# A four-engine transformer block: GpSimd rounds the feed-forward weights, one bias comes as a late column, and all instruction orders are laid anew

## What is computed

```python
# attention-like part
def _mlp(x, w1, b1, w2, b2): return _gelu(x @ w1 + b1) @ w2 + b2
n  = _ln(x, ln_g, ln_b)
W1 = _mlp(n, h1_w1, h1_b1, h1_w2, h1_b2)          # 128 -> 512 -> 128
W2 = _mlp(n, h2_w1, h2_b1, h2_w2, h2_b2)
W3 = jnp.tril(jnp.einsum('bzn,bsn->bzs', W1, W2))
t  = _ln(_gelu(jnp.einsum('bzs,bsm->bzm', W3, n)), ln_g, ln_b)
x1 = x + t
out = x + _mlp(_ln(x1, ln_g, ln_b), fm_w1, fm_b1, fm_w2, fm_b2)
# feed-forward part; the weights hold only -1, 0, 1, the *_s are scales by output feature
h = silu(tlin(x, w1_w, w1_s)) * tlin(x, w2_w, w2_s)
h = gelu(tlin(h, h1_w, h1_s)); h = gelu(tlin(h, h2_w, h2_s)); y = tlin(h, w3_w, w3_s)
# the block
x = x + _layernorm(attn(_layernorm(x)));  x = x + _layernorm(ffn(_layernorm(x)))
```

## Time and profile before

| | us |
|---|---|
| median of 3 runs | 365.95 (365.81 to 366.39) |
| span of the profiled execution, first to last instruction | 362.6 |
| the median less the span | 3.4 |
| PE busy in the span | 350.1 (97%) |
| DVE busy | 319.9 (88%) |
| ACT busy | 305.2 (84%) |
| GpSimd busy | 147.2 (41%) |

### The profile page before, as it was taken

The page is one execution under the profiler, slowest core; times in us unless marked ns, Lnnn a source line. Parts: engine busy times, 40 slices in busy tenths (PEclk is TensorE's granted clock), DMA queues, the critical chain, the costliest instruction groups (busy, mean ns, idle before and its releaser), DMA issues.

```text
span 362.6 us, 6039 instructions
## 1 busy us (share of the span) xinstructions
PE 350.1 (97%) x1788; PEld 289.2 (80%) x1788; DVE 319.9 (88%) x954; ACT 305.2 (84%) x552; POOL 147.2 (41%) x213
## 2 busy tenths in 40 slices
...
DMA packets 8804, 9.08 MB, mean 25 GB/s; under 512 B 577, under 2 KB 6722, under 8 KB 8770
## 3 DMA queue, kind: packets, MB, share of 16 engines
...
## 4 chain that ended last, share of the span: by engine, by line
PE 67%; ACT 13%; DVE 10%; issue 5%; DMA 2%; POOL 1%; SPq 1%; POOLq 0%; DVEq 0%; ACTq 0%
PE bank L1224 8%; PE bank L1226 8%; PE bank L1240 6%; PE bank L1241 6%; PE bank L1123 4%; PE bank L1104 4%; PE bank L1108 4%; PE bank L1105 4%; PE bank L1120 4%; PE bank L1121 4%; PE bank L1206 4%; PE bank L1209 4%; ACT h_hidden_hi L510 3%; PE bank L1046 2%; ACT bank L515 2%
## 5 line engine op out<-in xcount | busy, mean ns | idle before, releaser
L715 DVE TENSOR_TENSOR ffn_gate_lo<-bank,ffn_gate_hi 128x512 fp32r<-128x512 f32 (+1 forms) x72 | 44.1, 626 | 6.0 <-ACT bank L584 4.9
L510 ACT ACTIVATE h_hidden_hi<-bank,cols 128x512 fp32r<-128x512 f32 x64 | 46.1, 760 | 3.5 <-PE bank L1108 3.2
L515 ACT ACTIVATE bank<-bank,cols 128x512 f32<-128x512 f32 x64 | 45.1, 739 | 0.3
L715 DVE TENSOR_TENSOR h_hidden_lo<-bank,h_hidden_hi 128x512 fp32r<-128x512 f32 x64 | 43.0, 681 | 2.5 <-ACT bank L515 2.5
L584 ACT ACTIVATE bank<-bank,cols 128x512 f32<-128x512 f32 (+1 forms) x72 | 43.7, 620 | 0.7
L1224 PE MATMUL bank<-ffn_gate_hi,ffn_w_hi 128*128 128x512 f32 (+1 forms) x108 | 40.5, 381 | 0.2 <-DVE ffn_gate_lo L715 0.2
L1226 PE MATMUL bank<-ffn_gate_lo,ffn_w_hi 128*128 128x512 f32 (+1 forms) x108 | 39.3, 370 | 0.2 <-DVE ffn_gate_lo L715 0.2
L578 ACT ACTIVATE ffn_h_hi<-bank,cols 128x512 fp32r<-128x512 f32 (+1 forms) x36 | 23.0, 646 | 13.5 <-PE bank L1226 8.3
L578 ACT ACTIVATE ffn_gate_hi<-bank,cols 128x512 fp32r<-128x512 f32 (+1 forms) x36 | 23.2, 647 | 10.6 <-PE bank L1226 8.3
L364 POOL TENSOR_TENSOR XR<-X,ln_x_r 128x512 f32<-128x512 f32 x8 | 8.3, 1042 | 53.6 <-DVE bank L861 53.4
L715 DVE TENSOR_TENSOR ffn_h_lo<-bank,ffn_h_hi 128x512 fp32r<-128x512 f32 (+1 forms) x36 | 22.0, 626 | 8.0 <-ACT bank L584 7.8
...
## 6 DMA issues: line engine op xcount, KB each, us to landing
raw<-ffn_w SPq DMA_DIRECT2D x5, 512.0 KB, 3.9
...
```

The source lines that it names most:

```text
L510: nc.scalar.activation(dst, bank(f"{L}u{j}", c)[:, :], ACT.Gelu, bias=bias_of(L, j)).then_inc(*hi[L].done(c, j))
L515: nc.scalar.activation(u[:, :], u[:, :], ACT.Gelu, bias=bias_of(L, j)).then_inc(*act2[L].done(c, j))
L715: return nc.vector.tensor_tensor(dst, whole, high.bitcast(f32), ALU.subtract)
```

## The change

Four things are done.

- `ffn_w_hi` moves from ACT to GpSimd, as `tensor_copy` (six instructions). Behind each stand the blocks that it feeds.
- `fm_b2` is loaded as a column of 128 values of 4 bytes, straight into its tile. The DMA is issued after `x_piece(2)` in place of before `x_piece(1)`. The two 1x1 matmuls and DVE's copy are gone; `fm_evict(0)` waits for the DMA.
- All orders are laid anew, on all engines, and with them `TURNS`. On PE `fm_bias_product` comes after `down_mm("h1", 2, 0)`; `n_transpose(1)` comes before the last of the h2 layer; `down_mm("h2", 3, 3)` comes before the branch.
- Among what is laid anew is what GpSimd runs around DVE's `n_first` and `n_second`; there `t_r(0)` and `n_low(1)`, for instance, have changed neighbours.

```diff
-        b2_row = M[0:1, 0, :]
...
-            sp.dma_start(b2_row, rows[2:3, :]).then_inc(b2_in, 16)
             x_piece(1, 1, 2)
             for i in (3, 4, 5):
                 attn_piece(i)
             x_piece(2, 2, 3)
+            sp.dma_start(fm_b2[:, :], rows[2:3, :].rearrange("o d -> d o")).then_inc(b2_in, 16)
...
+            def ffn_w_hi(i):
+                c0, c1, at = F_PIECES[i]
+                pool.wait_ge(ffn_in[i], 16)
+                nc.gpsimd.tensor_copy(Fw[0][:, c0:c1], raw[:, at:at + c1 - c0]).then_inc(*ffn_hi.done(0, i))
...
-            x_s_(0); n_low(0); x_s_(1); x_s_(2); lo_block(0); lo_block(1); x_r(0); xr_scale(0); lo_block(2); xr_b(0)
-            lo_block(3); n_low(1); t_r(0); x_r(1); lo_block(4); lo_block(5); x1_r(0); lo_block(6); lo_block(7); x_s_(3)
-            lo_block(8); n_low(2); t_r(1); xr_scale(1); xr_b(1); lo_block(9); o_r(0); x_r(2); x1_r(1); lo_block(10); y_r(0)
+            x_s_(0); n_low(0); x_s_(1); ffn_w_hi(0); lo_block(0); x_s_(2); x_r(0); ffn_w_hi(1); lo_block(1); lo_block(2)
+            xr_scale(0); xr_b(0); ffn_w_hi(2); n_low(1); t_r(0); lo_block(3); lo_block(4); lo_block(5); x1_r(0)
+            ffn_w_hi(3); x_r(1); ffn_w_hi(4); lo_block(6); x_s_(3); ffn_w_hi(5); lo_block(7); n_low(2); t_r(1); x_s_(4)
+            lo_block(8); xr_scale(1); xr_b(1); lo_block(9); o_r(0); lo_block(10); x1_r(1); x_r(2); y_centre(0); y_r(0)
...
-            up_act("h2", 1, 0); up_hi("h2", 3, 0); nT_high(1); up_act("h2", 2, 0); up_act("h2", 3, 0); ffn_w_hi(0)
-            attn_w_hi(5); down_hi("h1", 0); down_hi("h2", 0); up_hi("h1", 0, 1); up_hi("h2", 0, 1); ffn_w_hi(1)
+            up_hi("h2", 2, 0); up_act("h2", 1, 0); up_act("h2", 2, 0); up_hi("h2", 3, 0); up_act("h2", 3, 0); nT_high(1)
+            down_hi("h1", 0); attn_w_hi(5); down_hi("h2", 0); up_hi("h1", 0, 1); up_hi("h2", 0, 1); up_hi("h1", 1, 1)
...
-                nc.vector.tensor_scalar(fm_b2[:, :], bank("fb", 0)[:, J:J + 1], 1.0, None, ALU.mult)
...
-            x_st(0); x_ag(0); n_first(0); n_second(0); attn_w_lo(0); attn_w_lo(1); nT_low(0); x_st(1); x_ag(1); n_first(1)
-            attn_w_lo(2); attn_w_lo(3); up_lo("h1", 0, 0); up_lo("h1", 1, 0); n_second(1); up_lo("h1", 2, 0); up_lo("h2", 0, 0)
-            x_st(2); up_lo("h1", 3, 0); x_ag(2); up_lo("h2", 1, 0); nT_low(1); up_lo("h2", 2, 0); up_lo("h2", 3, 0)
-            attn_w_lo(4); down_lo("h1", 0); down_lo("h2", 0); attn_w_lo(5); fm_bias_add(); score_mask(0, 0); score_mask(1, 0)
-            score_lo(0, 0); score_lo(1, 0); up_lo("h2", 0, 1); up_lo("h1", 0, 1); up_lo("h1", 1, 1); up_lo("h1", 2, 1); x_st(3)
-            t_st(0); n_first(2); t_ag(0); n_second(2); up_lo("h2", 1, 1); t_gain(0); up_lo("h1", 3, 1); nT_low(2); x1_sum(0)
+            x_st(0); x_ag(0); n_first(0); n_second(0); attn_w_lo(0); attn_w_lo(1); nT_low(0); x_st(1); x_ag(1)
+            attn_w_lo(2); n_first(1); n_second(1); up_lo("h1", 0, 0); up_lo("h1", 1, 0); x_st(2); up_lo("h1", 2, 0)
+            attn_w_lo(3); up_lo("h2", 0, 0); up_lo("h1", 3, 0); attn_w_lo(4); up_lo("h2", 1, 0); x_ag(2)
+            up_lo("h2", 2, 0); up_lo("h2", 3, 0); nT_low(1); down_lo("h1", 0); down_lo("h2", 0); attn_w_lo(5); x_st(3)
+            score_mask(0, 0); score_mask(1, 0); score_lo(0, 0); score_lo(1, 0); up_lo("h2", 0, 1); up_lo("h1", 0, 1)
+            up_lo("h1", 1, 1); gate_constants(); up_lo("h1", 2, 1); x_ag(3); t_st(0); t_ag(0); n_first(2)
+            up_lo("h2", 1, 1); n_second(2); up_lo("h1", 3, 1); t_gain(0); nT_low(2); x1_sum(0); up_lo("h2", 2, 1)
...
-                pe.wait_ge(b2_in, 16)
-                last = nc.tensor.matmul(bank("fb", 0)[:, J:J + 1], b2_row, ones[0:1, :], start=True, stop=True)
```

More of the change, by code:

```diff
@@ L436, in _ @@
[L436 to L440, removed]
@@ new lines, in _ @@
+            ffn_w_hi(3); x_r(1); ffn_w_hi(4); lo_block(6); x_s_(3); ffn_w_hi(5); lo_block(7); n_low(2); t_r(1); x_s_(4)
+            lo_block(8); xr_scale(1); xr_b(1); lo_block(9); o_r(0); lo_block(10); x1_r(1); x_r(2); y_centre(0); y_r(0)
+            y_scale(0); o_shift_(0); n_low(3); o_r(1); xr_scale(2); xr_b(2); t_r(2); n_low(4); x1_r(2); y_r(1)
+            y_centre(1); y_scale(1); x_r(3); x_s_(5); o_shift_(1); xr_scale(3); t_r(3); xr_b(3); f_r(0); x_r(4); x1_r(3)
+            o_r(2); y_centre(2); y_r(2); y_scale(2); f_r(1); xr_scale(4); t_r(4); xr_b(4); x_end(0); o_shift_(2); o_r(3)
@@ new lines, in _ @@
+            x1_r(4); x_s_(6); n_low(5); y_r(3); x_r(5); y_centre(3); y_scale(3); o_shift_(3); o_r(4); xr_scale(5); xr_b(5)
+            x_r(6); x_s_(7); y_centre(4); y_r(4); t_r(5); y_scale(4); n_low(6); x1_r(5); x_end(1); f_r(2); f_r(3)
+            x_end(2); xr_scale(6); o_shift_(4); o_r(5); t_r(6); xr_b(6); x_end(3); x_r(7); y_centre(5); y_r(5); y_scale(5)
+            o_shift_(5); n_low(7); x1_r(6); xr_scale(7); o_r(6); xr_b(7); t_r(7); f_r(4); y_centre(6); y_r(6); y_scale(6)
+            o_shift_(6); x1_r(7); o_r(7); o_shift_(7); y_r(7); y_centre(7); y_scale(7); f_r(5); x_end(4); f_r(6); x_end(5)
@@ L445, in _ @@
+            x_shift(); x_end(6); last_rstd(0); last_rstd(1)
         @block.scalar
@@ L609, in _ @@
-            attn_w_hi(5); down_hi("h1", 0); down_hi("h2", 0); up_hi("h1", 0, 1); up_hi("h2", 0, 1); ffn_w_hi(1)
-            up_act("h2", 0, 1); score_hi(0, 0); up_hi("h1", 1, 1); score_hi(1, 0); up_hi("h1", 2, 1); up_act("h1", 0, 1)
-            up_act("h1", 1, 1); up_act("h1", 2, 1); n_high(1); t_act(0); lo_sum(0); lo_sum(1); up_hi("h2", 1, 1); ffn_w_hi(2)
-            up_act("h2", 1, 1); up_hi("h1", 3, 1); up_hi("h2", 2, 1); up_act("h1", 3, 1); nT_high(2); ffn_w_hi(3)
-            up_act("h2", 2, 1); up_hi("h2", 3, 1); down_hi("h1", 1); up_hi("h1", 0, 2); up_act("h2", 3, 1); ffn_w_hi(4)
@@ L689, in _ @@
[L689 to L693 removed]
+            rows_out(); attn_w_hi(0); attn_w_hi(1); attn_w_hi(2); nT_high(0); n_high(0); attn_w_hi(3); up_hi("h1", 0, 0)
@@ new lines, in _ @@
+            up_act("h1", 2, 1); t_act(0); n_high(1); up_hi("h2", 1, 1); lo_sum(0); up_act("h2", 1, 1); up_hi("h2", 2, 1)
+            up_hi("h1", 3, 1); up_act("h1", 3, 1); up_hi("h2", 3, 1); up_act("h2", 2, 1); nT_high(2); up_act("h2", 3, 1)
+            lo_sum(1); up_hi("h1", 0, 2); down_hi("h1", 1); up_act("h1", 0, 2); up_hi("h1", 1, 2); up_hi("h1", 2, 2)
+            up_act("h1", 1, 2); up_act("h1", 2, 2); down_hi("h2", 1); up_hi("h2", 0, 2); lo_sum(2); mT_high(0)
+            up_act("h2", 0, 2); score_hi(0, 1); up_hi("h1", 3, 2); up_hi("h2", 1, 2); score_hi(1, 1); up_hi("fm", 0, 0)
@@ new lines, in _ @@
+            up_act("h1", 3, 2); up_act("fm", 0, 0); up_act("h2", 1, 2); t_act(1); n_high(2); up_hi("fm", 1, 0)
+            up_act("fm", 1, 0); up_hi("h2", 2, 2); up_hi("fm", 2, 0); up_act("h2", 2, 2); up_act("fm", 2, 0)
+            up_hi("fm", 3, 0); up_hi("h2", 3, 2); up_act("fm", 3, 0); up_act("h2", 3, 2); lo_sum(3); nT_high(3)
+            fm_evict(0); down_hi("h1", 2); up_hi("h1", 0, 3); up_hi("h1", 1, 3); up_act("h1", 0, 3); up_act("h1", 1, 3)
+            lo_sum(4); down_hi("h2", 2); up_hi("h1", 2, 3); up_hi("h1", 3, 3); up_act("h1", 2, 3); up_act("h1", 3, 3)
@@ new lines, in _ @@
+            up_hi("h2", 0, 3); up_hi("h2", 1, 3); lo_sum(5); up_hi("h2", 2, 3); up_act("h2", 0, 3); up_act("h2", 1, 3)
+            mT_high(1); up_act("h2", 2, 3); up_hi("h2", 3, 3); score_hi(0, 2); down_hi("h1", 3); up_act("h2", 3, 3)
+            score_hi(1, 2); up_hi("fm", 0, 1); up_hi("fm", 1, 1); up_act("fm", 0, 1); n_high(3); yT_high(0)
+            up_act("fm", 1, 1); down_hi("h2", 3); up_hi("fm", 2, 1); gate_tanh(0, 0); t_act(2); up_hi("fm", 3, 1)
+            gate_tanh(1, 0); up_act("fm", 2, 1); gate_hi(0, 0); up_act("fm", 3, 1); gate_hi(1, 0); nT_high(4)
@@ L971, in _ @@
-            up_lo("h1", 3, 2); t_st(1); up_lo("fm", 0, 0); n_first(3); up_lo("fm", 1, 0); n_second(3); t_ag(1)
-            up_lo("fm", 2, 0); up_lo("h2", 2, 2); up_lo("fm", 3, 0); t_gain(1); nT_low(3); x_st(5); branch(0)
-            up_lo("h2", 3, 2); o_st(0); down_lo("h1", 2); up_lo("h1", 0, 3); down_lo("h2", 2); o_ag(0); x1_sum(1)
-            up_lo("h1", 1, 3); x1_st(1); up_lo("h2", 0, 3); x1_ag(1); up_lo("h1", 2, 3); x_branch(0); m_norm(1); y_st(0)
-            up_lo("h1", 3, 3); y_ag(0); up_lo("h2", 1, 3); mT_low(1); score_mask(0, 2); up_lo("h2", 2, 3); score_mask(1, 2)
@@ new lines, in _ @@
+            yT_low(0); up_lo("fm", 1, 1); n_first(4); down_lo("h2", 3); gate_1(0, 0); n_second(4); gate_1(1, 0)
+            gate_2(0, 0); up_lo("fm", 2, 1); gate_2(1, 0); up_lo("fm", 3, 1); gate_lo(0, 0); gate_lo(1, 0); gate_1(2, 0)
+            nT_low(4); score_mask(0, 3); gate_2(2, 0); gate_1(3, 0); score_lo(0, 3); gate_lo(2, 0); gate_2(3, 0); t_st(2)
+            gate_lo(3, 0); score_mask(1, 3); branch(1); score_lo(1, 3); o_st(1); o_ag(1); t_ag(2); layer_lo("a", 0, 0)
+            up_lo("h1", 0, 4); t_gain(2); layer_lo("a", 1, 0); x_branch(1); layer_lo("a", 2, 0); up_lo("h1", 1, 4)
```

515 lines of the change are left out of this document (255 added, 260 removed), and 45 rows, old and new, of the table TURNS.

## The result

The changed kernel takes 368.67 us (median of 5 runs, 368.18 to 371.01) beside 365.81 us for the kernel before on the same chip (median of 5, 363.63 to 366.39). The two medians are 2.9 us apart; the ratio taken over all of these runs is 1.0109, 95% interval 1.0076 to 1.0142, and stands for 4.0 us. The forecast was 364.0 us, range 361.7 to 366.8. The profiled execution has a span of 366.9 us, 4.3 more than before. In all five runs of the changed kernel the time is 1.7 to 1.8 us above the span, not 3.4; so the profiled execution of the kernel before (span 362.6) was probably one of about 364.4 us, faster than its median, and spans overstate the loss a little.

The account below looks back on a forecast made before the run. ACT was taken to bound the first stage, DVE close behind, and PE the rest. A gain of 2.2 us less 0.25 for shared reads gave 2.0 us, so 364.0 us, range 361.7 to 366.8.

Parts of the forecast that it names:

- What bounds the kernel: From 10 to 73 us ACT is full with DVE close behind; from 73 to 281 us PE is the bound.
- ACT's relief: Roundings leaving ACT between 20.8 and 58.7 us free 5.2 us there; 2.2 us gained, limited by DVE's 3.8 us idle.
- GpSimd's copies: Six roundings on GpSimd, 1.5 us per 1024 columns (1.0 to 2.1): from 20 to 52 us full, but not late.
- The shared reads: DVE's attn_w_lo(5) and one n_second would likely meet GpSimd reads of SBUF: 0.25 us lost, bound 1.3 us each meeting.
- rival D: GpSimd copies block attn_w_lo(5), n_second(1) and n_second(2) on DVE, 1.3 us each, 3.9 in all: 367.7 us, chance 0.13.
- The new orders: All engines' new orders carry the same work: taken as 0, at most 0.7 us won or about 0.8 lost.
- The bias column: Dropping bias work on PE and DVE off the chain, with a hidden DMA: taken as 0, earlier DMAs 0 to 0.4.
- After 73 us: PE is nearly always busy; the stage only starts earlier if the first ends earlier, some 2 us.
- The base and its spread: Profiled span 362.6 us, median 365.95 us, their 3.4 us difference kept; earlier runs spread by 0.58 us.

Follow-up runs that it names:

- e11: The changed kernel with the six roundings back at their old places on ScalarE, plus the two moves of e4: 366.86 us, ratio 1.0042 to the kernel before.
- e6: e4 with one wait more, so that GpSimd begins its first rounding only when n_second(1) has ended: 363.35 us, ratio 0.994 to the kernel before.
- e4: The changed kernel with GpSimd's x_r(1) ahead of lo_block(3) and VectorE's n_second(2) ahead of up_lo(h2,1,1): 364.18 us, ratio 0.998 to the kernel before.
- f2: The kernel before with only the six roundings moved to GpSimd, each right ahead of its first block, other orders kept: 364.81 us, ratio 0.9977.
- e3: The changed kernel with the six roundings back at their old places on ScalarE: 369.95 us, ratio 1.0131 to the kernel before.

## Why the prediction was wrong

- **What bounds the kernel: right. ACT's relief: right in kind, too small by over a third.** ACT lost 5.5 x 0.95 us of work, and e11 against e6 puts the worth of that at 3.7 us, where the forecast had 2.2; that is close to its bound, DVE's 3.8 us of idle time. The 2.2 us between e11 and e4 match the forecast by chance, since the meeting of `n_second(1)` is taken off them. The worth is there only where the orders can use it: f2, in the old ones, had 0.8.
- **GpSimd's copies: the mechanism right, the size below the estimate.** 1.04 us for 1024 columns and 0.61 for 512 (estimate 1.5, bounds 1.0 to 2.1). `n_low(1)` ended at 32.53 us, forecast 32.1. The Trainium skill's figure ("GPSIMD Engine Reference", section 3.1) would have given an estimate of 1.54 us; the measurement decides. In the changed kernel GpSimd was not late; f2 alone shows VectorE waiting for it, 0.5 us more than before.
- **The shared reads, taken at 0.25 us: this step failed.** The runs put the two meetings at 4.7 us (the change against e4, with the clock) and 1.5 us (e4 against e6). It failed in four ways. The price was 0.25 us, taken from one row in which an instruction began 0.39 us before a block ended; the bound, one whole GpSimd instruction, was the price. The count was one price for each step, where a step has four instructions and each can pay: five lost 0.78 and 1.08 us at 12.7 to 15.1, and 0.93, 1.00 and 1.00 us at 34.9 to 38.7, 4.8 us together. `attn_w_lo(5)`, which I had counted on, lost nothing, since it began first and GpSimd's block waited instead (3.02 us for two). And the place was misread: against rival D stood that `n_second(2)` has the short `t_r(0)` beside it. `up_lo` stands ahead of it, and when that was done `t_r(0)` had ended 0.1 us before. The order could have told it: three blocks follow one another there. Last, the readers were the wrong ones: the forecast counted the six moved roundings, but it was three blocks, on GpSimd before and after, that held `n_second(2)`, and e3 has that meeting without a rounding on GpSimd. The Trainium skill's rule ("SBUF — State Buffer", "Who interferes with whom"), that the later one is blocked for the whole of the other, was cited, but it went only into the bound and rival D, not into the sum; the traces agree with it (4.92 us for 1.12).
- **Rival D named the mechanism**, at 367.7 us and a chance of 0.13: whole instructions of waiting, 3.9 us in all for the 4.8 measured. That it comes out within 1 us of 368.67 is partly luck: one of its three steps lost nothing, the largest met blocks and not copies, its relief was 2.2 for 3.7 us, and it had no clock. Of the 3.5 us between the spans of the change and e4, TensorE's idle time at 34 to 42 us is 3.38 - 1.44 = 1.9, and the lower clock with what follows the other 1.6, by difference; 3.4 us at half speed, 1.7, agree.
- **The new orders, taken at 0 with a bound of 0.8: wrong.** They carry the same work, but they laid three blocks beside `n_second(2)`, which costs 4.7 us. Apart from that e11 has +1.5 us (0.8 to 2.3) while ScalarE is full; which of the many moves costs this stays open. In the other direction they are what lets the rounding's move give 3.7 us and not 0.8 (f2).
- **The bias column: taken at 0, measured 0.7 us faster** (interval 0.1 to 1.4), with the cause open. The DMA took 5.6 us to land, hidden, as said.
- **After 73 us: right.** TensorE idles 0.33 us of 208; the gap carried over is that of the first stage.
- **The base and its spread.** The 3.4 us between span and median belong to two different executions; taken within one, it is 1.8 us. The forecast is none the worse, as it comes to the median less 2.0 us. But the 0.58 us of spread came from three runs; 24 of them lie from 363.6 to 366.6 us.
